# PSUM banks of second heads, and the order of the last slots, in a two-layer transformer kernel

## The reference

```python
def _L1_attn_ref(x, Wq, bq, Wk, bk, Wv, bv, Wo, bo):      # 16 heads of 16
    a = jnp.einsum('blhd,bLhd->bhlL', q, k) * (1.0 / DHEAD)
    a = jax.nn.softmax(a, axis=-1)
    prefinal = jnp.einsum('bhlL,bLhd->blhd', a, v)
    out = prefinal.reshape(b, l, HEADS * DHEAD) @ Wo + bo
def _L1_ffn_ref(...):                                      # 256 -> 1024 -> 256
    x = fwht(x * SU_ug) / SCALE
    x = jax.nn.silu(x_gate) * x_up                         # after two products with weights
    x = fwht(x * SU_dp) / SCALE
    x = x @ W_down.T * (Wscale_dp * SCALE)
x = L0_attn_query
xn = _layernorm(x, axis=-1)
x = x + _L0_attn_ref(xn, ...) + _L0_ffn_ref(xn, ...)       # 16 causal heads of 128
xn = _layernorm(x, axis=-1)
x = x + _L1_attn_ref(xn, ...) + _L1_ffn_ref(xn, ...)
```

## Time and profile before

| | us |
|---|---|
| median of 3 runs (lowest, highest) | 988.21 (987.48, 988.67) |
| the profiled execution's own time | 989.46 |
| its span in the trace | 987.5 |
| mean clock granted to TensorE, share of full | 0.978 |

### The profile page before, as it was taken

How to read it: one execution, slowest core, us unless ns; L and a number is a source line. 1 busy time by engine, 2 the same in 40 slices (tenths; PEclk the granted TensorE clock), 3 DMA queues, 4 the chain that set the end, 5 groups by cost and what they waited for, 6 DMA issues and landing times.

```text
span 987.5 us, 22866 instructions
## 1 busy us (share of the span) xinstructions
PE 905.1 (92%) x8032; PEld 724.6 (73%) x8032; DVE 753.9 (76%) x2128; ACT 680.5 (69%) x1997; POOL 347.0 (35%) x637
## 2 busy tenths in 40 slices
PE   4786889899999999999999999999999999886887
PEld 2344667677788788887888788888888888765665
DVE  6886677667887888888888878788888888766466
ACT  4786786557767776777677777777677767755454
POOL 5502456424333333333333333333333333333242
PEclk9998999999999999999999999999999999989799
DMA  9243260002000100010002000200020001000000
GB/s 309 78 150 96 91 209 2 2 22 60 2 2 23 48 23 2 23 50 23 1 3 70 1 23 2 66 7 23 2 62 10 23 2 39 22 23 1 2 12 12
DMA packets 46880, 39.98 MB, mean 40 GB/s; under 512 B 4400, under 2 KB 42032, under 8 KB 46512
## 3 DMA queue, kind: packets, MB, share of 16 engines
q1 hardware_dynamic: 46768, 38.52, 12.7%
HBM read 30.11 MB, written 8.39 MB: 39 GB/s over the span
## 4 chain that ended last, share of the span: by engine, by line
PE 60%; DVE 18%; ACT 10%; issue 4%; ACTq 0%; DVEq 0%
PE ps L819 32%; PE ps L941 6%; ACT arena L1162 5%; DVE arena L812 5%; PE ps L869 5%; DVE arena L813 4%; PE ps L1040 3%; PE ps L1058 3%; PE ps L841 3%; ACT arena L808 3%; DVE arena L1321 3%; PE ps L902 2%; ACT arena L807 2%; PE ps L1069 2%; PE ps L1042 1%
## 5 line engine op out<-in xcount | busy, mean ns | idle before, releaser
L813 DVE SCALAR_TENSOR_TENSOR arena<-ps,bqk,arena 128x256 bf16<-128x256 f32 x416 | 187.5, 480 | 77.0 <-ACT arena L808 77.0
L808 ACT ACTIVATE arena<-ps,bqk 128x256 bf16<-128x256 f32 x416 | 177.8, 463 | 82.4 <-PE ps L1042 64.0
L812 DVE TENSOR_TENSOR arena<-ps,arena 128x512 bf16<-128x512 f32 (+1 forms) x336 | 204.4, 633 | 35.3 <-ACT arena L807 35.0
L819 PE MATMUL ps<-arena,wqkv 128*128 128x256 bf16 x1728 | 216.9, 276 | 0.3 <-DVE arena L812 0.3
L807 ACT ACTIVATE arena<-ps 128x512 bf16<-128x512 f32 (+1 forms) x336 | 181.0, 558 | 47.6 <-PE ps L869 30.3
L1552 POOL TENSOR_SCALAR arena<-arena,rc 128x128 f32<-128x128 f32 (+1 forms) x256 | 105.5, 425 | 273.2 <-DVE rc L1350 273.1
L1162 ACT ACTIVATE arena<-arena,nb 128x128 f32<-128x128 f32 (+1 forms) x256 | 114.4, 447 | 126.3 <-DVE nb L1321 126.2
L1559 POOL TENSOR_SCALAR arena<-arena,rc 128x256 f32<-128x256 f32 x254 | 118.2, 478 | 232.1 <-DVE rc L1354 232.1
L819 PEld LDWEIGHTS ps<-arena,wqkv 128*128 128x128 bf16 x1728 | 171.5, 99 | 24.5 <-issue 0.8
L1162 ACT ACTIVATE arena<-ps,nb 128x256 f32<-128x256 f32 x256 | 119.3, 478 | 16.3 <-DVE nb L1328 16.3
L819 PE MATMUL ps<-arena 128*128 128x128 bf16 (+2 forms) x864 | 98.4, 251 | 16.7 <-DVE arena L813 6.5
(11 more groups left out here) (115 smaller groups left out, 1283.6 us busy)
## 6 DMA issues: line engine op xcount, KB each, us to landing
scratch_qk<-arena SPq DMA_DIRECT2D x28, 128.0 KB, 1.9
arena<-scratch_qk SPq DMA_DIRECT2D x84, 32.0 KB, 1.8
arena<-scratch_qk SPq DMA_DIRECT2D x42, 64.0 KB, 2.5
arena<-in_x SPq DMA_DIRECT2D x4, 512.0 KB, 9.7
arena<-in_w_gating SPq DMA_DIRECT2D x4, 512.0 KB, 7.7
arena<-in_w_q SPq DMA_DIRECT2D x4, 512.0 KB, 4.6
arena<-in_w_k SPq DMA_DIRECT2D x4, 512.0 KB, 5.6
arena<-in_w_v SPq DMA_DIRECT2D x2, 1024.0 KB, 6.5
```

Source lines behind the costliest of these rows:

```text
L808: return nc.scalar.activation(out, in_, ACT.Identity, bias=bias)
L812: return nc.vector.tensor_tensor(out, in_, hi, ALU.subtract)
L813: return nc.vector.scalar_tensor_tensor(out=out, in0=in_, scalar=bias, in1=hi, op0=ALU.add, op1=ALU.subtract)
L819: last = nc.tensor.matmul(out, lhsT, rhs, start=(n == 0), stop=(n == len(steps) - 1))
```

## The change

Two parts. First, banks. A second head that is scored before slot NG0 = 128 stays in BK_M, and from slot 128 on it is scored in BK_QK. A second head that is turned before slot 128 is turned in BK_QK, between two uses of it for q and k, and from slot 128 on it is turned in BK_S. With that come other waits: `turn1` waits for `qk0_lo` of its slot (BK_QK) or for the last `p0_lo` (BK_S) where it waited for `exp1`, `proj_qk0` waits for `p1_lo` of a head that was turned there the slot before, and `scores1` in BK_QK waits for the last `qk0_lo` and for `p1_lo` of what was turned there. The waits for BK_M and for the turned head in BK_S1 fall away. The banks of the last batch stay as they are.

Second, the order in slots 134 and on. TensorE scored both heads of a slot, turned both of the slot before, and then made `up_gate`; now it scores and turns the first, makes `up_gate`, and scores and turns the second. ScalarE's `gate_tanh` goes from the slot's start to behind the first head's exponentials. VectorE's first reciprocal goes from behind `hidden` to ahead of it. GpSimd and SP have the same instructions in the same order. No instruction is added or taken out.

```diff
--- before.py
+++ after.py
@@ -688,12 +688,16 @@
             b, h = divmod(n, H1)
             if b == LASTB:
                 return (BK_S1, BK_S)[h % 2]
-            return BK_M if second(n) else BK_S1
+            if second(n):
+                return BK_M if head_slot(n) < NG0 else BK_QK
+            return BK_S1
 
         def turn1_bank(n):
 
             if n < LASTB * H1:
-                return BK_S1 if second(n) else BK_O
+                if second(n):
+                    return BK_QK if head_slot(n) + 1 < NG0 else BK_S
+                return BK_O
             if n % 2 == 0:
                 return BK_O
             return BK_X if head_slot(n) + 1 < END + 3 else BK_Y
@@ -853,9 +857,8 @@
                     pe.wait_ge(p1_lo, before[-1] + 1)
                 if bank == BK_QK:
                     pe.wait_ge(qk0_lo, min(slot + 1, NG0))
-                elif bank == BK_S1:
-                    pe.wait_ge(exp1, 1 + max(m for m in range(B * H1)
-                                             if score1_bank(m) == BK_S1 and head_slot(m) <= slot))
+                elif bank == BK_S:
+                    pe.wait_ge(p0_lo, NG0)
                 elif bank == BK_X or bank == BK_O and n >= LASTB * H1:
                     pe.wait_ge(qkv1_lo, 3 * B)
                 elif bank == BK_O:
@@ -890,6 +893,8 @@
                     pe.wait_ge(p1_lo, turned[-1] + 1)
                 if bank == BK_M:
                     free_m(pe, 0, n)
+                if bank == BK_QK:
+                    pe.wait_ge(qk0_lo, NG0)
                 if b == LASTB:
                     m, r = divmod(h // 2, 4)
                     rows32 = slice(32 * r, 32 * r + 32)
@@ -912,6 +917,9 @@
                     pe.wait_ge(cur_ready[b % 2], 16 * (b // 2))
                 if b == 0 and g % 4 == 0:
                     weights_ready(pe, ("qk", g // 4))
+                turned = [m for m in range(B * H1) if turn1_bank(m) == BK_QK and head_slot(m) + 1 < n]
+                if turned:
+                    pe.wait_ge(p1_lo, turned[-1] + 1)
                 for w in range(2):
                     last = group(ps[:, BK_QK, w * T:(w + 1) * T],
                                  [(wqkv0[:, a, w, k, g * HD0:(g + 1) * HD0], cur[:, b % 2, c, k, :])
@@ -1143,12 +1151,14 @@
                     pe_linear0(pe, PAIRS - 1, s - 4)
 
             for s in range(END, y_slot(LASTB)):
-                for n in heads_in[s]:
-                    scores1(n)
-                for n in heads_in[s - 1]:
-                    turn1(n)
-                for n in hidden_in[s]:
-                    up_gate(n, s)
+                for e in range(2):
+                    for n in heads_in[s][e:e + 1]:
+                        scores1(n)
+                    for n in heads_in[s - 1][e:e + 1]:
+                        turn1(n)
+                    if e == 0:
+                        for n in hidden_in[s]:
+                            up_gate(n, s)
                 for n in downs_in[s]:
                     down(n)
                 for n in outs_in[s]:
@@ -1295,13 +1305,14 @@
             for s in range(END, y_slot(LASTB)):
                 for n in quads_in[s - 1]:
                     o1_high(n)
-                for n in hidden_in[s - 1]:
-                    gate_tanh(n)
                 for e in range(2):
                     for n in heads_in[s - 1][e:e + 1]:
                         p1_high(n)
                     for n in heads_in[s][e:e + 1]:
                         exp_1(n)
+                    if e == 0:
+                        for n in hidden_in[s - 1]:
+                            gate_tanh(n)
 
         def dve_program(dve):
             def o0_low(n):
@@ -1534,11 +1545,11 @@
                         max_1(n)
                     for n in heads_in[s - 1][e:e + 1]:
                         p1_low(n)
+                    for n in heads_in[s][e:e + 1]:
+                        rec_1(n)
                     if e == 0:
                         for n in hidden_in[s - 1]:
                             hidden(n)
-                    for n in heads_in[s][e:e + 1]:
-                        rec_1(n)
                 if B * H1 - 1 in heads_in[s]:
                     norm_1(B * H1 - 1)
                 for b in y_in[s]:
```

## The result

The changed kernel takes a median of 982.36 us (977.78 to 983.58, seven runs) against 988.60 (987.30 to 992.28) for the kernel before on the same chip. The ratio is 0.9925, with a 95% interval of 0.9905 to 0.9944: faster, inside the range that was forecast, and 4.6 us slower than its point, 977.8. It lies 0.14 us inside the upper end of the range, 982.5.

The account below looks back on a forecast made before the run. TensorE was taken as the bound up to slot 124, and rings of waits between engines after it. Gains of 3.3, 1.6 and 2.3 (7.2) plus 3.2 made 10.4 us, off a median of 988.21: 977.8, range 974.5 to 982.5.

Parts of the forecast that it names:

- Slots 124 to 127: Second heads turned without waiting for the first head's exponentials; a gain of 0.2 us, bounds 1.5 and -1.0.
- wrong if q and k wait over 1 us: Sign against the forecast: q and k of slots 126 and 127 waiting over 1 us.
- Slot 128: Second score no longer waits for BK_M, so `hidden` comes at 889.0, not 892.34: 3.3 us gained.
- Slots 129 to 131: Three waits fall and x1 is summed earlier; a gain of 1.6 us, bounds 0 and 2.
- Slots 131 to 133: `transpose_x1` no longer stands behind the turned second head, so `p1_high` comes at 919.2, not 921.49: 2.3 us gained.
- The last batch: Second maxima of slot 141 at 973.07 against 976.27 under the new order; 3.2 us gained, bounds 0 and 4.2.
- The ring: Cycle of waits between engines in the last slots: 5.65 us a slot before; then 4.98, or 5.66 in slots 138 and 140.
- Rival 1: Only the banks pay: in the last slots `hidden` behind tanh makes 5.65 us a slot again; 981.0 us, 14%.
- rival 2: The banks pay half: x1 stays where it is in slots 129 to 133; 981.7 us, 14%.
- Rival 3: With the 3.36 us wait gone, the 24 projections run at full clock, 1.8 us more gain; 976.0 us, 10%.
- Rival 4: TensorE's clock falls in the last slots and the kernel is slower; 1004.4 us if in all six periods, 4%.
- Rival 5: Q and k of slots 126 and 127 waiting for VectorE cost what slot 128 gives; 986 to 989 us, 3%.

Follow-up runs that it names:

- turn_late: The changed kernel with the second heads of slots 124 to 126 turned in BK_S1 as before; 980.73 us, ratio 0.9928 to the kernel before.
- score_banks: The changed kernel with every second head turned in BK_S1 again; only the second scores from slot 128 on stay in BK_QK; 983.22 us, ratio 0.994.
- o1_res_later: The changed kernel with o1_low and the result of batch 6 moved later in VectorE's list in the last batch; 980.29 us, ratio 0.9923.
- the second comparison: The changed kernel, unaltered, run again against the kernel before; 982.91 us, ratio 0.9932.
- order_only: The kernel before with only the new order from slot 134 on, banks as before; 987.37 us, ratio 0.9986.
- best: The changed kernel with the edits of warm and o1_res_later; 978.13 us, ratio 0.9894 to the kernel before.
- best_all: The changed kernel with the edits of warm, o1_res_later and setup_warm; 978.04 us, ratio 0.9895 to the kernel before.
- banks_only: The changed kernel with the new banks kept and the last batch's order put back; 981.31 us, ratio 0.9931 to the kernel before.
- before_again: The kernel before, unaltered, run again on the same chip; 988.01 us, ratio 0.9989.
- warm: The changed kernel with 23 matmuls that nobody reads where TensorE waits in slots 131 and 132; 980.27 us, ratio 0.9923.
- setup_warm: The changed kernel with six matmuls without use ahead of one tile of each later pair in the setup; 980.42 us, ratio 0.9918.

## Why the prediction was right, and where it was off

**Slots 124 to 127**, 0.2 us: 0.25 in the trace, 0.2 in `turn_late`. Its sign "wrong if q and k wait over 1 us" came up (1.28 in slot 127) and meant nothing: the 1.00 us wait two groups later went. A bound on one wait is a poor sign where the wait can change places with another.

**Slot 128**, 3.3: measured 3.38 to `hidden`. The prediction gave TensorE 1.0 us for `turn0` and `project_out0`, its time at full clock, without saying that before they ran at half; it did run at full. **Slots 129 to 131**, 1.6: at the sum of x1 the gain was 910.11 - 905.15 = 4.96, so 1.58 more. **Slots 131 to 133**, 2.3: at the projections it was 923.07 - 915.86 = 7.21, so 2.25 more. The first part, 7.2 forecast, is right in each term against the trace that it was worked out from; against the two later traces of the kernel before the whole is 6.0 and 6.3. `score_banks` shows which bank carries which. Walking VectorE's and ScalarE's lists with the latencies of the trace was what gave this: the idle times of TensorE that went (1.5, 3.36 and parts of others) add up to another number.

**The last batch**, 3.2: this step failed in size. At slot 141 the gain was 976.27 - 966.54 = 9.73, so 2.52 from here. The ring's six slots went from 35.12 to 32.38, 2.74 for the forecast 3.05; its links of 4.98 and 5.66 were right (5.00, 5.70), but the first period is 5.31 for the forecast 5.2. The way into it, from the projections to the second maxima of slot 135, was to get 0.15 shorter and got 0.22 longer (18.08 to 18.30): the second score of slot 134 now stands behind `up_gate`, and its maxima wait 0.23. "TensorE's own work in a slot is 5.0" was 5.2 to 5.3 (`o1_res_later`). The base held more than the order: 1.2 of the 35.12 us are the fall of the clock at the earlier trace rows. The prediction had the row in hand (2.73 against 1.47), used it only for the danger of the rival, and never asked whether the new order, which closes the gap ahead of it, would be rid of it, or whether the next trace would show it. It came in all three traces of the kernel before, so a part of the 2.74 rests on a fact that the forecast held but did not use. Against the two later traces the last batch gains only 1.4 and 1.7, with the same ring: there the projections got the full clock back sooner (3.39 and 3.67 us for 4.41 and, changed, 4.57).

**The sum**, 10.4: 9.73 came about in the pair of traces, but the median moved by 6.2. The step that failed is the tacit one, that everything ahead of slot 124 keeps its time. In the trace of after it came 2.9 later. Over all comparisons the kernel before has a mean of 988.7 us in 72 runs and the changed one 981.9 in 13: 6.7 us. The late part alone, from the traces, is worth 7.4 to 9.7. That the range held is in part luck: the measured 982.36 lies outside the 975.5 to 980.0 that the forecast had by its own, and the second comparison's 982.91 would have missed the range.

**The rivals.** Rival 1, only the banks pay (981.0), and rival 2, half of them (981.7), both give a number nearer to the median than the forecast's, and both for a wrong reason: the ring did shorten, and the sum of x1 and the projections have the whole 7.2. Rival 3 did not come about, though its 1.8 us is real. Rival 4 did not come about: 43 us at a clock of 1.00. But neither did its condition, a stop in each half of a slot: from 931 to 970 us TensorE waited only twice, 0.16 and 0.33 us. The section "A second HAM failure mode: psum-queue depth-cycling" of the Trainium skill's "TensorE: Matmul & The Clock Gate", on which the prediction's warning rests, was therefore not put to the test. And the "many" gaps of the trace of before that went with the full clock are three, of 0.40 to 0.50 us. Rival 5 is refuted by the interval.

**What stays open.** Whether the late setup belongs to the changed program or to chance. Its traces and that of `order_only` had 2.9 to 3.0 us, `best` and `best_all` 2.3 to 2.4, five other variants of it 0.6 to 1.4, `banks_only` 0.07, and the three traces of the kernel before (one with its setup filled) 0 to 0.9. That may be a property of the program, but each is one execution, and the courses are shared: near 81 us `before_again` is 1.1 late and four variants of the changed kernel 0.9 to 1.2, `banks_only` 0.02, and the page of `before_again` has the third slice of the clock at 7 as well. The mean granted clock divides the runs into a few groups: of the changed kernel's 13 runs eight lie near 983.0 us with 0.977, four near 980.8 with 0.981 to 0.983, one at 977.8 with 0.988; the kernel before has 992.3 with 0.972, 990.0 with 0.977, 989.2 with 0.979, most often 987.6 with 0.981 or 0.982, and once 984.0 with 0.988. At one mean clock the two kernels are thus 6.2 to 7.0 us apart. What decides how often the clock falls in an unchanged stretch wasn't found, and the one try at steadying it failed.

## What to carry to other kernels

Walk the lists of the engines that release the bound one, with measured latencies from link to link; a wait that goes is worth the distance to what comes late next, here 1.86 of 3.36 us. Before taking a period from the trace as the cost of an order, see whether the same matmuls take one duration all through it. Where they don't, price the stretch at the lower clock apart and look for it in a second trace: here it came with a wait of 1.7 us in three traces of four, and went with the wait in all ten. And where an edit is worth under 1%, take two traces of the kernel before at least, and compare stretches with the unchanged part ahead of them taken off, since medians alone put 0 on a part that was worth 1.7 us.

## What the runs showed of the hardware

- TensorE's clock falls or does not after the same wait. Twelve matmuls behind a gap of 1.70 or 1.71 us took 2.73, 2.24 and 2.48 us in three traces of the kernel before and 1.47 in that of `banks_only`, with the same instructions there; behind a gap of 2.12 or 2.13 six took 0.82 (the changed kernel) or 1.27 (`warm`).
- The unchanged code ahead of slot 124 came up to 3.0 us later from trace to trace, with other granted clocks in 35 to 75 us (0.66 for 0.83, 0.83 for 1.00), and the times of one kernel fall into groups some 2 us apart, each with its own mean clock.
- Matmuls whose result nobody reads, put where TensorE waits, kept it at 2.4 GHz through 904 to 920 us, in the second half of which the granted clock had been 0.51, and cost nothing on the path: 24 projections 2.78 us for 4.57. In the setup the same means moved the fall elsewhere (0.83 in 65 to 75 us in `setup_warm`) and gained nothing that shows.
- Where the tile of the array changes from one group of matmuls to the next, the next starts 0.1 us later: 0.75 or 0.76 us behind the start of a group of six, for 0.65 or 0.66 with the same tile.
